# Self-attention with cosine-grouped normalisation: score tiles in two 64-row tiles of the array, and straight code in place of a loop

## The reference

```python
x_f = einsum('oc,bcn->bon', Wf, xf) + bf       # 16 channels
x_g = einsum('oc,bcn->bon', Wg, xf) + bg       # 16 channels
x_h = einsum('oc,bcn->bon', Wh, xf) + bh       # 128 channels
s = einsum('bci,bcj->bij', x_f, x_g)           # 1024 x 1024 per image
beta = softmax(s, axis=-1)
y = x + gamma * einsum('bci,bij->bcj', x_h, beta)
# then: cosine of the channels of y over all images, the 3 nearest-to-orthogonal
# partners of each channel (top_k of -|cos|), mean and variance over a channel and
# its partners for each image, and gamma * (y - mean) * rsqrt(var + eps) + beta
```

## Time and profile before

| | |
|---|---|
| median of three runs | 214.68 us (214.36 to 214.85) |
| span of the profiled execution | 211.9 us |
| median less span | 2.8 us |
| TensorE (PE) busy | 186.4 us, 88% of the span |
| VectorE (DVE) busy | 173.7 us, 82% |
| ScalarE (ACT) busy | 143.9 us, 68% |
| GpSimd (POOL) busy | 34.3 us, 16% |

### The profile page before, as it was taken

How to read it: one execution, slowest core, us unless ns; L and a number is a source line. 1 busy time by engine, 2 the same in 40 slices (tenths; PEclk the granted TensorE clock), 3 DMA queues, 4 the chain that set the end, 5 groups by cost and what they waited for, 6 DMA issues and landing times.

```text
span 211.9 us, 2596 instructions
## 1 busy us (share of the span) xinstructions
PE 186.4 (88%) x727; PEld 115.2 (54%) x727; DVE 173.7 (82%) x317; ACT 143.9 (68%) x256; POOL 34.3 (16%) x39
## 2 busy tenths in 40 slices
PE   7669979999999999999999999999999999983100
PEld 3435546465765676466756675657465756462000
DVE  6588989979898889979797979887988898766660
ACT  2548976799379955995499658984799378740320
POOL 0200210034003400160007100520034001001400
PEclk9999999999999999999999999999999999997555
DMA  6240002500060007000520052002200020000198
GB/s 207 89 162 0 0 0 100 203 0 0 39 257 3 0 0 292 6 0 3 205 94 0 0 186 111 0 0 99 99 0 0 3 99 0 0 0 0 53 403 336
DMA packets 4904, 16.16 MB, mean 76 GB/s; under 512 B 544, under 2 KB 672, under 8 KB 4896
## 3 DMA queue, kind: packets, MB, share of 16 engines
q1 hardware_dynamic: 4320, 14.68, 18.4%
q10 hardware_dynamic: 576, 1.38, 1.7%
HBM read 4.52 MB, written 4.19 MB: 41 GB/s over the span
## 4 chain that ended last, share of the span: by engine, by line
PE 71%; DVE 13%; ACT 6%; issue 5%; POOL 1%; DVEq 0%; ACTq 0%; POOLq 0%
PE o_ps L636 40%; PE s_ps L617 11%; PE w_ps L611 6%; PE w_ps L606 6%; DVE nmax L404 3%; PE w_ps L651 3%; ACT probs L318 3%; PE w_ps L645 2%; PE o_ps L603 2%; DVE y_all L596 1%; DVE probs_low L418 1%; DVE g_parts L427 1%; DVE y_cur L447 1%; ACT probs_high L324 1%; DVE values L435 1%
## 5 line engine op out<-in xcount | busy, mean ns | idle before, releaser
L318 ACT ACTIVATE probs<-s_ps,nmax 128x1024 f32<-128x1024 f32 x64 | 70.9, 1108 | 40.5 <-DVE nmax L404 40.5
L636 PE MATMUL o_ps<-probs,vnorm 128*128 128x512 f32 x192 | 90.2, 594 | 0.5 <-DVE y_cur L447 0.5
L404 DVE TENSOR_REDUCE nmax<-s_ps 128x1 f32<-128x1024 f32 x64 | 77.9, 1218 | 10.2 <-PE s_ps L617 9.8
L617 PE MATMUL s_ps<-g_parts,f_parts 128*128 128x512 f32 x128 | 51.6, 485 | 4.6 <-ACT probs L318 2.3
L636 PEld LDWEIGHTS o_ps<-probs,vnorm 128*128 128x128 f32 x192 | 35.3, 189 | 28.8 <-issue 23.2
L266 POOL TENSOR_TENSOR f_parts<-fg,fg_neg 64x512 fp32r<-64x512 f32 x14 | 24.0, 1713 | 122.1 <-ACT fg_neg L311 122.1
L617 PEld LDWEIGHTS s_ps<-g_parts,f_parts 128*128 128x128 f32 x128 | 21.2, 190 | 20.7 <-issue 14.0
L418 DVE TENSOR_TENSOR probs_low<-probs,probs_high 128x1024 fp32r<-128x1024 f32 x16 | 19.5, 1221 | 1.3 <-ACT probs_high L324 1.2
L427 DVE TENSOR_TENSOR g_parts<-fg,fg_neg 64x512 fp32r<-64x512 f32 x16 | 13.9, 871 | 6.6 <-ACT fg_neg L311 6.5
L335 ACT ACTIVATE vnorm<-values,rinv 128x128 f32<-128x128 f32 x48 | 18.8, 391 | 0.0
L611 PEld LDWEIGHTS w_ps<-wd,x_cur 128*128 128x128 f32 x112 | 14.7, 192 | 6.7 <-issue 6.7
(11 more groups left out here) (90 smaller groups left out, 165.7 us busy)
## 6 DMA issues: line engine op xcount, KB each, us to landing
x_all<-x_dram SPq DMA_DIRECT2D x7, 512.0 KB, 4.0
x_cur<-x_all SPq DMA_DIRECT2D x7, 512.0 KB, 3.2
y_all<-y_cur SPq DMA_DIRECT2D x7, 512.0 KB, 2.9
out_dram<-y_all SPq DMA_DIRECT2D x5, 512.0 KB, 5.8
out_dram<-y_all ACTq DMA_DIRECT2D x2, 512.0 KB, 4.1
x_all<-x_dram SPq DMA_DIRECT2D x2, 256.0 KB, 3.7
out_dram<-y_all SPq DMA_DIRECT2D x2, 256.0 KB, 2.2
wd<-wide_dram ACTq DMA_DIRECT2D x1, 256.0 KB, 4.3
```

The costliest lines, as they stand in the source:

```text
L318: nc.scalar.activation(probs[t][:, :], s_ps[t % 2][:, :], ACT.Exp, bias=nmax[:, t:t + 1], accum_out=rsum[:, t:t + 1]).then_inc(exp_done, 1)
L404: nc.vector.reduce_max(nmax[:, t:t + 1], s_ps[t % 2][:, :], AX_X, negate=True).then_inc(max_ready, 1)
L617: last = nc.tensor.matmul(s_ps[t % 2][:, h], f_parts[par][:, t * P:(t + 1) * P], g_parts[par][:, h], start=True, stop=True)
L636: last = nc.tensor.matmul(o_ps[:, halves[h]], weights[:, :], rows[:, halves[h]], start=(t == 0 and n == 0), stop=(t == T - 1 and n == len( ...
```

## The change

- The loop is gone: all eight stages are written out, each image's tiles are addressed directly, and `x_cur`, `y_cur` and their DMA copies are dropped, with the waits of the residual and of the last part on them.
- SP issues all loads of x at the start, those of images 2 to 7 after the constants have landed. Each image has a semaphore of its own.
- `g_parts` is now 512 columns wide: rows 0 to 63 hold the first 512 columns of g, rows 64 to 127 the other 512. There are no zeros, and their memsets are dropped.
- Rows 64 to 127 of `f_parts` hold a copy of rows 0 to 63. SP makes it by one DMA for each half (64 rows by 512 columns) after `f_ready`; for the first half of the first image VectorE computes it twice.
- The two matmuls of a score tile contract over 64 rows each: one uses rows 0 to 63 of the array, the other rows 64 to 127. They write the same two banks as before. All other matmuls stay as they are.
- The score of an image's first tile waits for the copy of the first half of f, that of its fifth tile for the copy of the second half.

```diff
-        g_parts = [sb(f"g_parts{i}", [P, N], F32R) for i in range(2)]
+        g_parts = [sb(f"g_parts{i}", [P, BANK], F32R) for i in range(2)]
...
+        def run_stages(stage):
+
+            for b in range(B):
+                stage(b, b % 2, first=b == 0, previous=b > 0, turn=b > 1, project=b < L)
...
+            for b in range(1, B):
+                if b == 2:
+
+                    sp.wait_ge(const_in, 16)
+                sp.dma_start(x_all[:, b, :], x[b]).then_inc(x_in[b], 16)
+            for b in range(B):
+                for h in range(H):
+                    if b == 0 and h == 0:
+                        continue
+                    sp.wait_ge(f_ready, H * b + h)
+                    sp.dma_start(f_parts[b % 2][KP:P, halves[h]].bitcast(F32),
+                                 f_parts[b % 2][0:KP, halves[h]].bitcast(F32)).then_inc(f_doubled[h], 16)
...
+            def parts_g(b, h):
+                parts(g_parts[b % 2][h * KP:(h + 1) * KP, :], g_rows, halves[h], g_ready)
...
-                if not first:
-
-                    dve.wait_ge(y_kept, 16 * b)
-                    dve.wait_ge(sq_ready, b)
-                    dve.wait_ge(yT_made, b)
...
-            for i in range(2):
-                nc.vector.memset(f_parts[i][KP:P, :].bitcast(F32), 0.0).then_inc(zeros_set, 1)
-                nc.vector.memset(g_parts[i][KP:P, :].bitcast(F32), 0.0).then_inc(zeros_set, 1)
...
-                    parts(f_parts[0], f_rows, halves[0], f_head)
+                    for rows in (slice(0, KP), slice(KP, P)):
+                        parts(f_parts[0][rows, halves[0]], f_rows, halves[0], f_head)
...
             def score(t, par):
-                for h in halves:
-                    last = nc.tensor.matmul(s_ps[t % 2][:, h], f_parts[par][:, t * P:(t + 1) * P],
-                                            g_parts[par][:, h], start=True, stop=True)
+                for h in range(H):
+                    rows = slice(h * KP, (h + 1) * KP)
+                    last = nc.tensor.matmul(s_ps[t % 2][:, halves[h]], f_parts[par][rows, t * P:(t + 1) * P],
+                                            g_parts[par][rows, :], start=True, stop=True)
...
                             pe.wait_ge(g_ready, H * (b + 2))
-                            pe.wait_ge(f_ready, H * b + 2)
+                            pe.wait_ge(f_doubled[0], 16 * (b + 1))
                         if t + AHEAD == TH:
 
-                            pe.wait_ge(f_ready, H * b + 1)
+                            pe.wait_ge(f_doubled[1], 16 * (b + 1))
```

More of the change, by code:

```diff
@@ L125, in build @@
         head_in = [sem("head_in0"), sem("head_in1")]
-        x_in = [sem("x_in0"), sem("x_in1")]
+        x_in = [None] + [sem(f"x_in{b}") for b in range(1, B)]
         table_in = sem("table_in")
@@ L336, in scale_values, with stage @@
                                      scale=rinv[:, t:t + 1]).then_inc(vn_ready, 1)
-            def stage(b, par, first=False, previous=True, turn=True, project=True, load_ahead=True, x_count=16):
+            def stage(b, par, first, previous, turn, project):
                 for t in range(T):
@@ L353, in stage @@
                         if first:
-                            act.wait_ge(f_head, 1)
+                            act.wait_ge(f_head, 2)
                         act.wait_ge(f_ready, H * b + 1)
@@ L371, in _ @@
                     scale_values(0, t - 1, 0, fresh=True)
-            run_stages(act, stage)
+            run_stages(stage)
             def square(h):
@@ L425, in parts @@
             def parts(to, rows, columns, done):
-                nc.vector.tensor_tensor(to[0:KP, columns], fg32[rows, columns], fg_neg[rows, columns].bitcast(F32),
+                nc.vector.tensor_tensor(to, fg32[rows, columns], fg_neg[rows, columns].bitcast(F32),
                                         ALU.add).then_inc(done, 1)
+            def parts_g(b, h):
+                parts(g_parts[b % 2][h * KP:(h + 1) * KP, :], g_rows, halves[h], g_ready)
             f_rows, g_rows = slice(0, KP), slice(KP, P)
@@ L437, in add_value_bias, with residual @@
                                         bias, ALU.add).then_inc(v_ready, 1)
-            def residual(b, first):
+            def residual(b):
                 dve.wait_ge(probs_used, T * (b + 1))
-                if not first:
-                    dve.wait_ge(y_kept, 16 * b)
-                    dve.wait_ge(sq_ready, b)
-                    dve.wait_ge(yT_made, b)
                 for h in range(H):
-                    nc.vector.scalar_tensor_tensor(y_cur[:, halves[h]], o_ps[:, halves[h]], wd[:, GAMMA:GAMMA + 1],
-                                                   image(x_all, b)[:, halves[h]], ALU.mult, ALU.add,
-                                                   accum_out=sums[:, h, bass.ds(b, 1)]).then_inc(y_ready, 1)
+                    nc.vector.scalar_tensor_tensor(y_all[:, b, halves[h]], o_ps[:, halves[h]], wd[:, GAMMA:GAMMA + 1],
+                                                   x_all[:, b, halves[h]], ALU.mult, ALU.add,
+                                                   accum_out=sums[:, h, b:b + 1]).then_inc(y_ready, 1)
             def low_part(tiles, source):
@@ L468, in add_gram, with stage @@
                 dve.wait_ge(gram_added, b + 1)
-                nc.vector.scalar_tensor_tensor(half_cos[:, :], turned, rnorm[:, bass.ds(b, 1)], half_cos[:, :],
+                nc.vector.scalar_tensor_tensor(half_cos[:, :], turned, rnorm[:, b:b + 1], half_cos[:, :],
                                                ALU.mult, ALU.add).then_inc(gram_added, 1)
-            def stage(b, par, first=False, previous=True, turn=True, project=True, load_ahead=True, x_count=16):
+            def stage(b, par, first, previous, turn, project):
                 for t in range(T):
@@ L486, in stage @@
                     if t == T - 1 and project:
-                        residual(b, first=first)
+                        residual(b)
                     if (project or t + SCALED < T) and (t + SCALED) % T in SPLIT:
@@ L495, in stage @@
                         dve.wait_ge(neg_ready, H * (b + 1) + t - 1)
-                        parts(g_parts[1 - par], g_rows, halves[t - 2], g_ready)
+                        parts_g(b + 1, t - 2)
             nc.vector.memset(warm[:, :], 0.0).then_inc(warm_set, 1)
-            for i in range(2):
-                nc.vector.memset(f_parts[i][KP:P, :].bitcast(F32), 0.0).then_inc(zeros_set, 1)
-                nc.vector.memset(g_parts[i][KP:P, :].bitcast(F32), 0.0).then_inc(zeros_set, 1)
             nc.vector.memset(half_cos[:, :], 0.0).then_inc(gram_added, 1)
@@ L505, in _ @@
                 dve.wait_ge(neg_ready, h + 1)
-                parts(g_parts[0], g_rows, halves[h], g_ready)
+                parts_g(0, h)
                 if h == 0:
-                    parts(f_parts[0], f_rows, halves[0], f_head)
+                    for rows in (slice(0, KP), slice(KP, P)):
+                        parts(f_parts[0][rows, halves[0]], f_rows, halves[0], f_head)
             dve.wait_ge(const_in, 16)
@@ L517, in _ @@
             nc.vector.tensor_copy(ident_b[:, :], ident).then_inc(ident_ready, 1)
-            run_stages(dve, stage)
+            run_stages(stage)
             for h in range(H):
@@ L605, in project_fg @@
             def project_fg(b, h):
-                return nc.tensor.matmul(w_ps[:, halves[h]], wd[:, WFG:WFG + P], image(x_all, b)[:, halves[h]],
+                return nc.tensor.matmul(w_ps[:, halves[h]], wd[:, WFG:WFG + P], x_all[:, b, halves[h]],
                                         start=True, stop=True)
@@ L675, in stage @@
                             pe.wait_ge(fg_copied, H * (b + 2))
-                        transposes(y_cur, w_ps, range(TH, T)).then_inc(yT_made, 1)
+                        transposes(y_all[:, b - 1, :], w_ps, range(TH, T)).then_inc(yT_made, 1)
                     if first and t == 0:
@@ L699, in stage @@
                             pe.wait_ge(gram_added, b)
-                        transposes(y_cur, w_ps, range(TH))
+                        transposes(y_all[:, b - 1, :], w_ps, range(TH))
                     if t in (5, 6) and project:
-                        pe.wait_ge(cur_in, 16 * (b + 1))
                         if previous:
@@ L737, in _ @@
             score(2, 0)
-            run_stages(pe, stage)
+            run_stages(stage)
             for h in range(H):
```

40 lines of the change are left out of this document (8 added, 32 removed).

## The result

The changed kernel takes 221.97 us (221.88 to 222.28, four runs) against 214.52 of the kernel before in the same comparison: a ratio of 1.0346, 95% interval 1.0331 to 1.0361. It is slower by 7.5 us; the forecast was 208.1, and 221.97 lies 1.0 above the upper end of the range, 221. The profiled execution has a span of 220.2 us and a time of 222.0, so 1.8 us lie around it. In the runs of the kernel before that list both, 2.1 to 2.6 us lie around the span, so the span has grown by more than the time: by 8.3 us, from 211.9.

A forecast was written before the change was run, and what follows sets the result against it. TensorE was taken to bound the middle stages, with VectorE next. The span of 211.9 us, less 7.1 for the middle, plus 0.5 for the start, gave 205.3; plus 2.8 around it, 208.1 us, range 204.9 to 221.

The forecast's parts named there:

- the cost of the score pair: TensorE's two score matmuls run at once, 0.23 us instead of 0.46, so its stage falls from 22.22 to 20.38 us.
- Nothing orders them: Reason given for 0.23 us a pair: its two matmuls use different rows, columns of g and banks.
- the first rival: Around each score pair, tiling changes cost more than the pair saves: 220.0 or 231.2 us; chance 0.27.
- threshold of 0.11 us a change: Price of one tiling change from which the chain's 51 score pairs no longer pay for the later start.
- gaps on TensorE: Sign of a wrong forecast: gaps before and after each score pair, with TensorE still on the chain.
- VectorE as the next bound: In middle stages VectorE's work and waits for ScalarE set a 20.58 us floor; 21.1 taken, saving 7.1 over 6.3 stages.
- The copy of f: Before an image's first score, the first half's DMA lands in 1.7 us, hidden with 0.14 us cover: no cost.
- The start: First image: VectorE's extra f instruction delays the start 0.7 us, one pair gives back 0.23: +0.5 us.
- The copy of the second half behind the loads: At the start this copy queues behind six 512 KB loads: nothing, or up to 1.2 us; nothing taken.
- What needed no price: Copies of x and y, their waits, memsets and the loop's turn are off the chain; nothing for longer code.
- the chain of the last stage: From 169.74 us on the stage belongs to VectorE and ScalarE, no engine full throughout, and stays as long.
- The time around the span: Outside the profiled span, 2.8 us by which the runs' median exceeds it, added to 205.3 for 208.1.

The follow-up runs named there:

- the run with half the scores: The straight kernel with only the first 512 columns of each score tile computed, the first image's two first tiles whole: 203.01 us.
- the straight kernel: The changed kernel with scores back on 128 rows, zeros set again at the start and no copy of f: 213.71 us.
- the runs with two tiles together: Two tiles' scores in every second step, on 64 rows and 128: 231.28 and 229.57 us; with VectorE's two maxima ahead of its other work, 220.40 and 221.38.

## Why the prediction was wrong

**The step that failed** is the cost of the score pair. It took 0.23 us for the pair with both halves at once, which is right, and nothing for going from tiles of 128 rows to 64 and back, which is wrong. "Nothing orders them" was argued from the two matmuls of a pair alone; the matmuls on either side of the pair were not part of the argument. The mechanism was the first rival, with a chance of 0.27, and its price had been bounded at 0.16 to 0.27 us a change from the earlier trace rows. The runs show 0.19. The pair with its two changes costs 0.23 + 0.38 = 0.61, 0.15 more than the 0.46 of before, and the chain shows 0.16, in two places. That rival's threshold of 0.11 us a change was passed clearly. With 0.15 its sum gives 51 x 0.15 + 0.7 = 8.4 us, a span of 220.3, where 220.2 was measured. That it fits so well is luck in part: 7.3 us fall in the middle, 0.3 before it and 0.7 in the last image. The sign that was named for it, gaps on TensorE, does not show, as its records overlap by 0.06 us at a change; the chain and the loads of weights show it.

The Trainium skill, in the page that was named there, "TensorEngine Tiling (Array Packing)", section "Tiling Modes", says that a change of mode drains TensorE. The traces agree, with 0.19 us each way, and with the loads of weights that wait for the end of the group before. The Trainium skill, page "TensorE: Matmul & The Clock Gate", section "Part 3: Packing small matmuls", has tiles in different rows start some 4 ns apart. The records agree as far as they tell: both matmuls of a pair end within 0.49 us, the length of one.

**VectorE as the next bound** was the right step, ScalarE being in the chain with it, with a term sized too large. 21.1 us a stage was taken, from a floor of 20.58; without changes of tiling it is 20.51. All of VectorE's waits for TensorE go, of which 0.3 us had been kept, and the waits for ScalarE stay, at 1.3 us where the floor had 1.1. That 20.51 lies so near the floor is luck in part, as VectorE's work in that window is 19.11 and not 19.48. The gain on the table was up to 10.7 us, not 7.1, and the change of tiling took it and 8.3 more.

**The copy of f** was costed at nothing and costs nothing here, but not for the reason given: it lands in 2.2 us and not in the estimated 1.7 (the first one, behind the loads, in 7.6). In the stage of 23.5 us there are 2.2 us between its landing and the score. In a stage of 20.5 us it would be about 0.1 us late: in the run with half the scores GpSimd ends the first half of f at 126.71 + 1.80 = 128.51, so that a copy would land at about 130.7, and the first score of the next image starts at 130.60. That was only worked out, not run.

**The start** came out as told in its parts, as against the straight kernel. VectorE makes `f_parts` twice, the second time beside GpSimd for 1.74 us, and the first score starts at 11.16 against 10.39 in the straight kernel: 0.77 later, 0.7 forecast. The answer to the earlier trace rows:

```profile
7.93 2.46 DVE L405 TENSOR_TENSOR f_parts<-fg,fg_neg 64x512 fp32r<-64x512 f32 x2
8.58 1.25 POOL L253 TENSOR_TENSOR f_parts<-fg,fg_neg 64x512 fp32r<-64x512 f32 x1 [7.76 <-ACT fg_neg L292]
...
10.42 0.69 DVE L405 TENSOR_TENSOR g_parts<-fg,fg_neg 64x512 fp32r<-64x512 f32 x1
```

In the kernel before the first score was at 11.19 all the same, since its first projection took 1.51 us on the chain against 0.97 in the changed kernel and 0.87 in the straight one. With one profile of each, why is open. It is not what the straight kernel gains: of the 0.8 us by which its first score is earlier, 0.1 is left where its middle begins, at 28.07 against 28.18. In the changed kernel the middle begins 0.3 later than before, where 0.5 was forecast. The copy of the second half behind the loads was in time: issued at 9.87, it landed at 17.5, and the fifth tile's score starts at 18.39.

**What needed no price**: the copies of x and y, the memsets, the loop. Right: the straight kernel shows 213.71, and stages of 22.22 us as before. That the chain of the last stage is VectorE's and ScalarE's was right for the kernel before, but that no engine is full there was misread: the last row has TensorE at 19.10 of 19.16 us. The slower TensorE has taken the stage over.

**The time around the span** was a term sized too large as well: 2.8 us was added, and 1.8 lie there.

## What to carry to other kernels

A matmul on part of the array is priced with its neighbours: count the changes of tile size in the order in which TensorE runs them, at 0.19 us each here, and compare with what the tile saves, 0.23 us for 512 columns. By these numbers tiles of 64 rows pay where several pairs stand together, and not where one pair stands between full matmuls: two pairs save 0.46 us for two changes of 0.19. That is worked out and not shown, as TensorE did not set the pace in the runs with two tiles together. Before such a change is built, leaving out the work that it would save tells in one run what the gain can be and which engine is next, and a small matmul of the other tile size, here of 256 columns, with a control on full rows tells the price.

## What the runs showed of the hardware

TensorE's clock can fall in a short wait, and need not. In the changed kernel TensorE has nothing between 8.3 and 11.16 us, and the windows that answer to the earlier trace rows show the granted clock (third column from the right) at 0.57 and 0.50, the lower level of 1.2 GHz:

```profile
11.00:12.00 1.00, 0.84 (x4) 0.50 (x4) 0.97 (x3) 0.00 (x0) 0.00 (x0) 0.57 1.00 389
12.00:13.00 1.00, 1.00 (x3) 0.50 (x2) 1.00 (x2) 0.00 (x0) 0.00 (x0) 0.50 0.97 332
```

In the kernel before it had nothing from 8.9 to 11.2 and kept 1.00. But the later start is not shown to be the cause, for the straight kernel has nothing only from 8.16 to 10.39, no longer than the kernel before, and its clock falls too:

```profile
11.00:12.00 1.00, 1.00 (x4) 0.75 (x3) 1.00 (x3) 0.00 (x0) 0.00 (x0) 0.62 1.05 418
12.00:13.00 1.00, 1.00 (x2) 0.34 (x1) 1.00 (x2) 0.18 (x1) 0.00 (x0) 0.50 0.99 401
```

These are single profiles, and what decides stays open. The cost is seen in the four projections behind the first scores: they take 3.01 us of the chain in the changed kernel and 3.22 in the straight one, where their records lasted 1.88 us together in the kernel before. So the third tile's score comes at 15.39 against 14.83, and the 0.23 us that the pair should have given back at the start does not show; the straight kernel's comes at 14.98, though its first score was 0.8 us earlier. The Trainium skill, page "TensorE: Matmul & The Clock Gate", section "Part 1: The HAM clock gate (the "warmup" mystery)", says that TensorE's clock is halved after it has been idle. The windows of these two kernels agree; those of the kernel before show no fall.

When VectorE and GpSimd add parts of `fg` and `fg_neg` at the same time, the one that starts second takes longer. In the stage of the kernel before, VectorE's `g_parts` starts at 111.81 and takes 0.69 us, and GpSimd's `f_parts` starts at 111.86 and takes 1.80. In the changed kernel GpSimd starts first, at 118.37, and takes 1.27, and VectorE, from 118.72, takes 1.48. In the start of the earlier trace rows it is 1.25 and 1.73.

A DMA of 128 KB inside the core takes 2.2 us to land, as long as a store of 256 KB: the two are of different kinds, but the estimate of 1.7 us, worked out from sizes alone, did not hold between them.
